# Second attention: each batch's row maxima are copied by ScalarE beside a constant one-hot pattern, and no longer moved by transfers; the first scores contract 64 rows, the second 88

## The reference, cut to what matters

```python
attn = jnp.einsum('bhnd,bhmd->bhnm', q, k) * SCALE     # 16 heads of 8, 256 tokens
attn = jax.nn.softmax(attn, axis=-1)
out  = jnp.einsum('bhnm,bhmd->bhnd', attn, v)
```

## Time and profile before

| | |
|---|---|
| median of 3 runs | 1743.43 us (1741.2 to 1749.72) |
| profiled execution, span from first to last instruction | 1814.1 us |
| TensorE busy, share of the span | 79% |
| ScalarE busy | 54% |
| mean granted TensorE clock of the span | 0.895 |
| second attention | from about 1180 us to 1760 us of the span |

### The profile page before, as it was taken

One profiled execution on the slowest core, in us unless ns is written; L12 is line 12 of the kernel. 1 busy time (PEld: TensorE's weight loads), 2 busy tenths in 40 slices (PEclk: granted clock), 3 DMA queues, 4 the chain that ended last, 5 costly groups with the idle time before them and its releaser, 6 DMA issues.

```text
span 1814.1 us, 32941 instructions
## 1 busy us (share of the span) xinstructions
PE 1434.0 (79%) x8094; PEld 974.1 (54%) x8094; DVE 1064.9 (59%) x3974; ACT 973.5 (54%) x2664; POOL 448.9 (25%) x495
## 2 busy tenths in 40 slices
PE   7999999999999999818999999125676667567581
PEld 4666665666665656416788888112344344335351
DVE  2677777777777777636443343025466556656555
ACT  6777777777777777414455555002344334334454
POOL 1012111222222212125100000665434433441003
PEclk9999999999999999859999999656788778878896
DMA  9000000000000000022122222144334333332301
GB/s 342 1 10 12 12 12 12 12 12 12 12 12 12 10 10 12 11 81 64 59 67 69 64 69 66 38 63 57 49 54 51 50 41 56 49 49 42 41 2 46
DMA packets 76443, 78.90 MB, mean 43 GB/s; under 512 B 10769, under 2 KB 69650, under 8 KB 75954
## 3 DMA queue, kind: packets, MB, share of 16 engines
q1 hardware_dynamic: 55378, 49.77, 13.9%
q0 software_dynamic: 8192, 16.79, 3.3%
q10 hardware_dynamic: 12816, 11.67, 1.9%
HBM read 47.92 MB, written 29.49 MB: 43 GB/s over the span
## 4 chain that ended last, share of the span: by engine, by line
PE 26%; DMA 11%; SPq 6%; issue 4%; DVE 3%; another core or an unknown queue 2%; ACT 1%; DVEq 1%; POOL 1%; POOLq 0%; ACTq 0%
PE psum L766 7%; PE psum L774 7%; DMA qst<-mrow 5%; SPq L425 3%; PE psum L810 3%; DMA wall<-mrow 3%; PE psum L799 2%; DMA qkd<-parts 2%; SPq L439 1%; PE psum L873 1%; PE psum L748 1%; PE psum L832 1%; PE psum L780 1%; POOL yk L543 1%
## 5 line engine op out<-in xcount | busy, mean ns | idle before, releaser
L947 ACT ACTIVATE P<-shifted,least 128x192 f32<-128x192 f32 (+1 forms) x512 | 240.9, 471 | 179.5 <-DVE least L1111 164.9
L1311 DVE TENSOR_REDUCE mx<-psum 128x2 f32<-128x512 f32 x256 | 165.6, 686 | 172.2 <-PE psum L873 128.3
L1010 ACT ACTIVATE wall<-psum 128x1024 f32<-128x1024 f32 x128 | 131.1, 1024 | 215.9 <-PE psum L799 153.2
L659 PE MATMUL psum<-kT,qT 128*128 128x384 f32 (+1 forms) x512 | 214.7, 542 | 0.0
L492 POOL DMA_INDIRECT xs<-x1c,pos x128 | 125.1, 978 | 335.2 <-DVE pos L1182 298.5
L1111 DVE CUSTOM_DVE_ANT_0 shifted<-psum,band 128x192 f32<-128x192 f32 (+1 forms) x512 | 170.6, 383 | 48.7 <-PE psum L659 32.9
L993 ACT ACTIVATE hid<-psum,wA 128x256 f32<-128x256 f32 x320 | 133.1, 471 | 66.3 <-PE psum L766 65.4
L766 PE MATMUL psum<-xgT,wA 128*128 128x256 f32 x640 | 157.5, 390 | 11.1 <-DVE xgT L1250 11.1
L674 PE MATMUL psum<-ident,P 128*128 128x128 f32 x1024 | 138.4, 278 | 18.7 <-DVE P L1104 18.6
L774 PE MATMUL psum<-hid,wB 128*128 128x256 f32 x640 | 151.4, 379 | 0.4 <-ACT yTe L997 0.4
L1104 DVE TENSOR_SCALAR P<-P,rinv 128x192 f32<-128x192 f32 (+1 forms) x512 | 145.1, 345 | 9.9
(11 more groups left out here) (244 smaller groups left out, 2649.6 us busy)
## 6 DMA issues: line engine op xcount, KB each, us to landing
xg<-xs SPq DMA_DIRECT2D x80, 128.0 KB, 2.0
ys<-yrow ACTq DMA_DIRECT2D x80, 128.0 KB, 1.7
wall<-in_wall SPq DMA_DIRECT2D x1, 8232.0 KB, 35.6
qkd<-parts SPq DMA_DIRECT2D x16, 384.0 KB
qst<-qkd SPq DMA_DIRECT2D x66, 64.0 KB
kst<-qkd SPq DMA_DIRECT2D x66, 64.0 KB
wall<-qkd SPq DMA_DIRECT2D x60, 64.0 KB
hT<-in_xT SPq DMA_DIRECT2D x4, 512.0 KB, 5.9
```

What stands on the lines that cost most here:

```text
L659: mm(bk[:, 0:2 * w].rearrange("q (h j) -> q h j", h=2), qT[:, p, it * 128:(it + 1) * 128], kT[:, p, :, 0:w], start=True, stop=True).then_i ...
L947: last = sc.activation(P[:, par, it, h, 0:w], shifted[:, par, it, h, 0:w], ACT.Exp, scale=-1.0, bias=least[:, par, n:n + 1], accum_out=row ...
L1010: sc.activation(pc[:, p % 4, :, :, :].rearrange("q h j n -> q (h j n)"), ST, ACT.Exp, scale=SCALE1).then_inc(s["exps1"], 1)
L1311: v.tensor_reduce(out=mx[:, :, h], in_=SB[(par + 1 + h) % 3].rearrange("q (i n) -> q i n", i=TT), axis=mybir.AxisListType.X, op=ALU.max).t ...
```

## The change

1. The 24 transposed rows of minus the maxima are no longer copied to `mrow` and moved by SP. ScalarE writes them straight to rows 64 to 87 of `qst`, the same 256 values for each of the 8 heads of the half (an output of 24 x 2048 instead of 24 x 256).
2. `kst` rows 64 to 87 hold a constant pattern: row 8k + j is one in the columns of head j and of head j + 8, and zero in the others. So each head's second scores pick its own three rows of the 24.
3. The second scores contract rows 0 to 87, the first scores rows 0 to 63 (the stack's 48 rows and 16 of zeros).
4. The zeroing transfer from `zst`, `mrow` and the semaphore `m_in` are gone; TensorE waits for the ScalarE copy through `free0` and `free1`.
5. GpSimd's preparation builds the pattern with `affine_select` and clears rows 32 to 63 alone.

```diff
@@ SP @@
             def attention(b, par):
-                if has(b, 0):
-                    maxima(b, TMB, par, 1, 2 * b + 1, H1 * (b + 1))
...
-                    sp.dma_start(qst[load][MROW:MROW + NPART, :, :], zst[:, :, :]).then_inc(s["stk"], 16)
-                if has(b, 1):
-                    maxima(b, TMA, (par + 1) % 3, 0, 2 * b + 2, H1 * (b + 1) + H1 // 2)
-
-            def maxima(b, use, slot, half, before, scored):
...
-                    sp.dma_start(qst[slot][MROW + k:MROW + k + 1, half * hh:half * hh + hh, :], mrow[k * hh:(k + 1) * hh, :]).then_inc(s["m_in"], 16)
@@ GpSimd @@
             def clear(k):
-                g.memset(qst[k][:, :, :].rearrange("q h n -> q (h n)").bitcast(fp32), 0.0)
-                g.memset(kst[k][:, :, :].rearrange("q h n -> q (h n)").bitcast(fp32), 0.0)
                 g.drain()
-                g.memset(kst[k][MROW:MROW + NPART, :, :], 1.0)
+                g.memset(qst[k][32:64, :, :].rearrange("q h n -> q (h n)").bitcast(fp32), 0.0)
+                g.memset(kst[k][32:64, :, :].rearrange("q h n -> q (h n)").bitcast(fp32), 0.0)
+
+            def select_rows():
...
+                g.memset(rows.rearrange("q h n -> q (h n)").bitcast(fp32), 0.0)
+                g.drain()
+                for half in range(2):
+                    r = rows[:, half * H1 // 2:(half + 1) * H1 // 2, :]
+                    for k in range(NPART):
+                        g.affine_select(out=r, in_=r, compare_op=ALU.not_equal, fill=1.0, base=-k * H1 // 2,
+                                        pattern=[[-1, H1 // 2], [0, N]], channel_multiplier=1)
+                        g.drain()
+
+            def select_copy(k):
+                g.drain()
+                g.tensor_copy(kst[k][MROW:MROW + NMAX, :, :].rearrange("q h n -> q (h n)").bitcast(fp32),
+                              kst[0][MROW:MROW + NMAX, :, :].rearrange("q h n -> q (h n)").bitcast(fp32))
@@ TensorE @@
                         if p % 4 == 0:
-                            need(pe, "m_in", 16 * NPART * (2 * b + (p // 4 + 1)))
+                            if p == 0:
+                                need_free(pe, b - 1, TMA, 1)
+                            else:
+                                need_free(pe, b, TMB, 1)
...
-                                last = mm(ST[:, (2 * k + jt) * N:(2 * k + jt + 1) * N], kst[par][:, 2 * p + k, jt * 128:(jt + 1) * 128],
-                                          qst[par][:, 2 * p + k, :], start=True, stop=True)
+                                last = mm(ST[:, (2 * k + jt) * N:(2 * k + jt + 1) * N], kst[par][0:MROW + NMAX, 2 * p + k, jt * 128:(jt + 1) * 128],
+                                          qst[par][0:MROW + NMAX, 2 * p + k, :], start=True, stop=True)
...
-                        last = mm(SB[(nxt + h) % 3][:, it * N:(it + 1) * N], qst[nxt][:, h, it * 128:(it + 1) * 128],
-                                  kst[nxt][:, h, :], start=True, stop=True)
+                        last = mm(SB[(nxt + h) % 3][:, it * N:(it + 1) * N], qst[nxt][0:MROW, h, it * 128:(it + 1) * 128],
+                                  kst[nxt][0:MROW, h, :], start=True, stop=True)
@@ ScalarE @@
-            def maxima_row(b, use, before):
+            def maxima_row(b, use, slot, half):
                 need_full(act, b, use)
-                need(act, "m_in", 16 * NPART * before)
-                sc.activation(mrow[:, :], shared(use).bitcast(bf16)[0:NPART * H1 // 2, 0:N], ACT.Copy).then_inc(s[f"free{use[0]}"], 1)
+                hh = H1 // 2
+                sc.activation(qst[slot][MROW:MROW + NMAX, half * hh:half * hh + hh, :],
+                              shared(use).bitcast(bf16)[0:NMAX, 0:N].rearrange("q (o n) -> q o n", o=1).to_broadcast([NMAX, hh, N]),
+                              ACT.Copy).then_inc(s[f"free{use[0]}"], 1)
```

More of the change, by code:

```diff
@@ L24 @@
 MROW = 64
+NMAX = NPART * H // 2
 BIG = 1.0e30
@@ L223, in build @@
         shift = qst[0][:, :, :].rearrange("q h n -> q (h n)").bitcast(fp32).rearrange("q (n e) -> q n e", e=E)
-        zst = sb("zst", [NPART, H, N], bf16)
         v32 = sb("v32", [128, 3, TT, H, 32])
@@ L239, in build @@
         nmx = sb("nmx", [128, TT, 2, NPART, H // 2], bf16)
-        mrow = sb("mrow", [NPART * H // 2, N], bf16)
         oTc = sb("oTc", [128, N])
@@ L276, in build @@
             cw_in lora_mm c_set cleared st_full exps1 s_full max_done pv_full o_free full0 full1 free0 free1 a1_ready parts_ready
-            qkd_out stk m_in nm_ready x2_ready x2_kept x3_ready x3_kept gate_act scan_done
+            qkd_out stk nm_ready x2_ready x2_kept x3_ready x3_kept gate_act scan_done
             yk_in comb_done var2_ready pow2_ready posc_ready state_mm state_ready h_pre h_pre_last last_sum var3_ready pow3_ready scale_ready h_act fin_ready out_done""".split()
@@ L317, in build @@
         PRODUCTS = [(0, 0), (0, 1), (0, 2), (1, 0), (1, 1), (2, 0)]
-        NSTK = 2 * len(PRODUCTS) + 1
+        NSTK = 2 * len(PRODUCTS)
         TO3, TMB, QK, TOT, VP, TO0, WO = (1, 0), (0, 0), (0, 1), (1, 1), (0, 2), (1, 2), (0, 3)
@@ L426, in attention @@
                                          qkd[part].rearrange("(h d) c -> d h c", d=DH1)[:, :, c0:c0 + N]).then_inc(s["stk"], 16)
-                    sp.dma_start(qst[load][MROW:MROW + NPART, :, :], zst[:, :, :]).then_inc(s["stk"], 16)
-                if has(b, 1):
-                    maxima(b, TMA, (par + 1) % 3, 0, 2 * b + 2, H1 * (b + 1) + H1 // 2)
-            def maxima(b, use, slot, half, before, scored):
-                need_alone(sp, f"free{use[0]}", tally[use[0]].before(b, use[1] + 1))
-                need_alone(sp, "s_full", scored)
-                need_alone(sp, "m_in", 16 * NPART * before)
-                hh = H1 // 2
-                for k in range(NPART):
-                    sp.dma_start(qst[slot][MROW + k:MROW + k + 1, half * hh:half * hh + hh, :], mrow[k * hh:(k + 1) * hh, :]).then_inc(s["m_in"], 16)
             sp.wait_ge(s["cleared"], 2)
@@ L500, in clear @@
             def clear(k):
-                g.memset(qst[k][:, :, :].rearrange("q h n -> q (h n)").bitcast(fp32), 0.0)
-                g.memset(kst[k][:, :, :].rearrange("q h n -> q (h n)").bitcast(fp32), 0.0)
                 g.drain()
-                g.memset(kst[k][MROW:MROW + NPART, :, :], 1.0)
+                g.memset(qst[k][32:64, :, :].rearrange("q h n -> q (h n)").bitcast(fp32), 0.0)
+                g.memset(kst[k][32:64, :, :].rearrange("q h n -> q (h n)").bitcast(fp32), 0.0)
+            def select_rows():
+                rows = kst[0][MROW:MROW + NMAX, :, :]
                 g.drain()
+                g.memset(rows.rearrange("q h n -> q (h n)").bitcast(fp32), 0.0)
[10 more added lines that the diff above has]
+                              kst[0][MROW:MROW + NMAX, :, :].rearrange("q h n -> q (h n)").bitcast(fp32))
             npos = B * TT * TOPK
@@ L525, in _ @@
                 clear(k)
-            g.memset(zst[:, :, :], 0.0)
+            select_rows()
+            select_copy(1)
             g.drain()
@@ L532, in _ @@
             clear(2)
+            select_copy(2)
             g.drain().then_inc(s["cleared"], 1)
@@ L1026, in attention @@
                     if p == 1 and has(b, 0):
-                        maxima_row(b, TMB, 2 * b + 1)
+                        maxima_row(b, TMB, par, 1)
                     if p == 1 and has(b, 2):
@@ L1041, in attention @@
                     if p == 5 and has(b, 1):
-                        maxima_row(b, TMA, 2 * b + 2)
+                        maxima_row(b, TMA, (par + 1) % 3, 0)
                     if p == 5 and (has(b, 3) or has(b, -1)):
```

## The result

| | median us | range | runs |
|---|---|---|---|
| before | 1746.58 | 1741.2 to 1753.58 | 4 |
| after | 1764.83 | 1760.04 to 1771.44 | 4 |

Ratio 1.0112, 95% interval 1.008 to 1.0145: the change makes the kernel 1.1% slower, where 1.5% faster was forecast (1743 to 1718 us), and the time lies above the range. Two later sets of runs gave 1.0109 [1.0062, 1.0156] and, on a chip where the kernel before takes 1814 us, 1.0165 [1.0109, 1.0221].

A forecast was written before the change was run, and what follows sets the result against it. Path taken as the stack's transfers, with TensorE waiting for the maxima at p=0. Terms -2.8 - 1.2 + 1.5 + 0.3 + 0.6 = -1.6 us a batch, -24 over 15 turns, about 1 more at the start: 1743 to 1718 us, range 1694 to 1752.

The forecast's parts named there:

- What the removal is worth: At p=0, maxima no longer awaited, zeroing and six small transfers gone: -2.8 - 1.2 us a batch.
- the 2.8 and the 1.2: 2.8 us: second scores and product with V run while the stack lands; 1.2 us: zeroing and small transfers gone.
- The timed runs near a cycle of 31.3 us: Timed runs have less lag than the profile and run near the batch cycle seen where GpSimd fetches nothing, 31.3 us.
- the 71 us: Profiled span of 1814.1 us above the median of 1743.43, taken as lag of the profiled execution, 37 us of it remote waits.
- writes 24 x 2048: ScalarE's copy at p=1 and p=5 takes 1.86 us against 0.36; +1.5 us a batch on the path, at p=1.
- 64-row tiles: Around first scores, 14 tile switches of 0.13 us a batch, 1.8 us of TensorE, two on the path at p=0: +0.3 us.
- TensorE's own arrival: At p=0 TensorE, later by copy and switches, asks for the stack 1 us late or less: +0.6 us a batch.
- No change: Lower clock after more idling at p=1, or VectorE's wait moving behind the copy, eats 1.6 us: 1740 us, chance 0.16.
- Slower, held back by the fetches: TensorE's signals at p=1 come only after GpSimd's last fetch, so earlier gains don't count: +14, 1757 us, chance 0.12.
- The signs listed in advance: No transfer wait at p=0, copy 1.8 to 1.9 us, p=1 wait up 1.5 us, 0.1 us gaps around first scores.
- 64-row matmuls take another time: One of the listed signs that the forecast is wrong; it had left a 64-row matmul at the same length.

The follow-up runs named there:

- two-step version with rows 96: The change with maxima at rows 96 to 119 and ScalarE copying 24x256 to a buffer, then spreading it to eight heads, against the kernel before: 1688.9 us, 0.9679.
- rows 96: The change with its long copy, maxima at rows 96 to 119, scores contracting 96 and 120 rows, against the kernel before: 0.9768 first chip, 0.9746 second.
- h3: The change with maxima at rows 96 to 119, first scores over 64 rows, second over 120, long copy, against the kernel before: 1794.7 us, 0.9895, second chip.
- e0: The kernel before, unchanged, profiled once more on the second chip: 1819.6 us.

## Why the prediction was wrong

*What the removal is worth: right.* It said -2.8 - 1.2 = -4.0 us a batch. The two-step version with rows 96 has the removal and next to none of the costs, and gains 56 us, over 15 turns 3.7 us a batch: two thirds of the 82.3 us waited for at p=0, and so less than all of it, as the prediction had it. How the gain splits into the 2.8 and the 1.2 was not tested.

*The timed runs near a cycle of 31.3 us: right, for a wrong reason.* They have no remote waits and a period of 31.6 us. But the 71 us were the chip's, not the profiled execution's.

*The copy, step "writes 24 x 2048": about right by itself.* 1.865 us was measured for each of the 32 copies, 1.86 predicted, and the wait at p=1 grew by the 1.5 us predicted (0.9 to 2.3 us a time on the first chip). Beside wide matmuls it costs 19 us, 1.3 a batch, where +1.5 was put. In the kernel before it cost 2.3 a batch; there the maxima's transfers leave later as well, which is a likely reason that was not tested.

*Step "64-row tiles": failed.* The gap per switch was right: in the change's timeline four first scores take 0.97 us from start to start in the slow clock, with rows 96 0.86. The sentence "a 64-row matmul itself I leave at the same length" is right at equal clock only (the shortest first scores take 269 ns with 64 rows, 270 with 96, 272 with 128). Two things were left out. The larger is the clock: with 64 and 88 rows it stayed low behind a wait where with 96 and 120 it came back. The 88 rows of the second scores had no term in the sum at all, and 120 in their place give back some 49 us on the second chip, over 3 us a batch. The smaller is that only two of the 14 switches were put on the path; the 27 us left there, 1.8 a batch, are in all likelihood the rest of them. The step was priced at +0.3; beside the long copy, both narrow contractions cost (1.0109 - 0.9768) x 1751 = 60 us, 4.0 a batch.

*Step "TensorE's own arrival" (+0.6): mis-sized by the same.* It added the two costs and kept each at its length in the clock of before. TensorE's busy time grew by 84 us (1409.7 in the kernel before, profiled on the first chip, to 1493.7), and the chain that ended last is now made of its rows in the main. The costs were predicted at 1.5 + 0.3 + 0.6 = 2.4 us a batch; measured 0.043 x 1745 / 15 = 5.0. With -3.7 that is +1.3, and 15 times that 19 us, the 1.1%.

*Rivals.* "No change" named the clock at p=1, but capped it at 1.6 us. "Slower, held back by the fetches" gave 1757, near in number by luck: its mechanism is not seen on the chip that was timed, which has no remote wait. The signs listed in advance came true (no transfer waits at p=0, copy 1.865 us, gaps of 0.1 us, wait at p=1 grown by 1.5); "64-row matmuls take another time" was the one that mattered, through the clock: their mean from 1200 us on is 345 ns where 269 is the shortest, against 297 in the kernel before.

*Open.* That the time and the clock move with the rows contracted is shown (88 against 120, with the maxima moved and nothing else of the stage changed), and since the rows added hold zeros, it is not their values. Whether the number of rows counts, or the 32-row strips that they touch, was not tried. That the switches are what is left between h3 and rows 96 is argued from their gaps. Why one kind of chip has the late signals is open.

## What to carry to other kernels

Price a wait put on a busy TensorE not by its length alone: see in the windows what the clock does after it, and how long until it is back. Free a shared PSUM bank with the smallest copy that does it and do the rest from SBUF, behind what others wait for; and let the instruction that waits stand behind independent matmuls. Here a narrower contraction saved nothing in a matmul's length and lost the clock; try it with the rows padded too, since beside a wait it cost far more than alone.

## What the runs showed of the hardware

- The granted clock of the stage (1240 to 1640 us) was 0.62, 0.67, 0.81 and 0.84 for 64+64, 64+88, 64+120 and 96+120 rows in first and second scores, all on one kind of chip and with the same copy; the first leaves the maxima out. After a wait at p=1 of some 2.3 us, on the other kind, it was back in 2.7 to 6.2 us with 96+120 rows and in 6 to 8.3 us with 64+88 (13 of 14 waits), read in slices of 1 us.
- A switch between 64-row and wider matmuls took 0.10 us (0.54 against 0.44 us from start to start for a group of four of 256 columns), and 0.11 us in the slow clock (0.97 against 0.86).
- The kernel before took 1745 to 1751 us in some sets of runs and 1806 to 1814 in others, each steady within 1.2%. In the second kind ScalarE's exponentials wait 22 to 38 us for late signals. In the kernel before there (e0), each of the 30 such waits of over 1 us, ScalarE's and VectorE's, ended during one of GpSimd's indirect transfers or within 1.8 us of its end; the first kind has the same transfers and no such wait. For the change on the second:

```profile
ACT wall L1014 <- remote: 35.0, 10, 4.5
```

- ScalarE's copy of 24x256 took 0.36 us, of 24x2048 bf16 1.865 us from PSUM (1865 ns each time) and 1.91 us from SBUF, so SBUF as a source was no faster.
